# Four background conditionings moved from the grouped attention into the low-rank mixture, with their results kept in DRAM

## The reference, cut to what matters

```python
x = x + L1_ffn(cond2(x, side, side, w, u, t))    # low-rank mixture of experts, conditioning 3
x = x + L2_attn(cond(x, side, side, w, u, t))    # grouped attention, conditioning 4
x = x + L2_ffn(cond2(...))                       # quantised feed-forward, conditioning 5
x = x + L3_attn(cond(...))                       # selective scan, conditioning 6
x = x + L3_ffn(cond2(...))                       # mixture, four experts a token, conditioning 7

def cond(r, k, v, w, u, time_emb):
    decay = exp(-exp(w)) * (0.5 + 0.5 * tf)
    ek = exp(min(k, 30)); ekv = ek * v
    # a = a * decay + ekv_t, b = b * decay + ek_t: scans over the tokens, forward and backward
    num = nf + nb - ekv + exp(min(u + k, 30)) * v
    den = df + db - ek + exp(min(u + k, 30))
    return sigmoid(r) * (num / max(den, 1e-8)) * (0.8 + 0.2 * tf)
```

## Time and profile before

| | us |
|---|---|
| median of 3 runs (2028.22 to 2039.93) | 2029.68 |
| the profiled execution | 2035.18 |
| its span | 2033.9 |

### The profile page before, as it was taken

One profiled execution on the slowest core, in us unless ns is written; L12 is line 12 of the kernel. 1 busy time (PEld: TensorE's weight loads), 2 busy tenths in 40 slices (PEclk: granted clock), 3 DMA queues, 4 the chain that ended last, 5 costly groups with the idle time before them and its releaser, 6 DMA issues.

```text
span 2033.9 us, 16567 instructions
## 1 busy us (share of the span) xinstructions
PE 1648.3 (81%) x5375; PEld 885.9 (44%) x5386; DVE 1279.3 (63%) x2046; ACT 913.6 (45%) x1581; POOL 357.1 (18%) x233
## 2 busy tenths in 40 slices
PE   0599788878877999986798989876667777689998
PEld 0255354436753434433344444432312332247776
DVE  7476346634433653546778787748768799955665
ACT  4311525433332211225878787734555453324444
POOL 5000032223100010000000000000025665502332
PEclk9975789988676999998899999876778899989999
DMA  2000076426003000001101010100100000021110
GB/s 86 0 1 1 0 261 217 155 64 104 1 1 126 0 0 0 0 1 55 47 1 44 1 44 1 39 33 17 44 0 0 1 0 0 0 68 44 53 47 27
DMA packets 40043, 80.68 MB, mean 40 GB/s; under 512 B 8882, under 2 KB 26116, under 8 KB 37398
## 3 DMA queue, kind: packets, MB, share of 16 engines
q1 hardware_dynamic: 34870, 53.93, 8.7%
q0 software_dynamic: 5088, 25.69, 3.6%
HBM read 71.34 MB, written 7.22 MB: 39 GB/s over the span
## 4 chain that ended last, share of the span: by engine, by line
PE 29%; DVE 12%; ACT 7%; issue 4%; POOL 2%; DMA 0%; PEldq 0%; POOLq 0%; DVEq 0%; SPq 0%; ACTq 0%; PEld 0%
PE bank L157 21%; PE bank L2510 3%; PE bank L1895 2%; POOL s_bu L2426 2%; DVE s_bu L2322 1%; DVE s_bu L2314 1%; DVE g_q L1593 1%; DVE g_turn L1591 1%; DVE g_turn L1592 1%; PE bank L2446 1%; PE bank L1885 1%; PE bank L1876 1%; DVE g_q L1597 1%; DVE g_rs L1584 1%; DVE q_g L2070 1%
## 5 line engine op out<-in xcount | busy, mean ns | idle before, releaser
L2426 POOL TENSOR_TENSOR s_bu<-s_rep,s_du 128x1024 f32<-128x1024 f32 x64 | 151.5, 2371 | 718.0 <-DVE s_du L2306 607.7
L2314 DVE TENSOR_TENSOR_SCAN s_bu<-bank,s_bu 128x1024 f32<-128x1024 f32 x64 | 146.0, 2282 | 21.1 <-ACT bank L2388 10.1
L2510 PE MATMUL bank<-s_bu,ident 128*128 128x512 f32 x256 | 132.8, 645 | 1.0 <-DVE s_dl L2263 0.3
L2388 ACT ACTIVATE bank<-s_dl,s_an 128x510 f32<-128x510 f32 x128 | 83.0, 682 | 106.3 <-DVE s_bu L2314 106.2
L157 PE MATMUL bank<-e_xs,e_wsp 128*128 128x512 f32 x528 | 127.8, 391 | 0.7 <-issue 0.7
L157 PEld LDWEIGHTS bank<-e_xs,e_wsp 128*128 128x128 f32 x528 | 99.0, 188 | 22.8 <-issue 1.9
L157 PE MATMUL bank<-r_am,r_b 128*128 128x512 f32 x240 | 108.8, 593 | 0.0
L157 PE MATMUL bank<-conditioned,g_wqk 128*128 128x512 f32 x160 | 88.2, 680 | 7.4 <-DVE g_wqk L1578 7.4
L2446 PE MATMUL bank<-s_bc,s_pick 96*128 96x512 bf16 x128 | 42.0, 412 | 56.9 <-DVE s_bu L2322 55.5
L1420 POOL TENSOR_TENSOR r_ys<-r_y,r_y 128x512 f32<-128x512 f32 x14 | 22.8, 1631 | 342.0 <-DVE r_y L1365 342.0
L2322 DVE TENSOR_TENSOR s_bu<-s_bu,bank 128x1024 f32<-128x1024 f32 x64 | 76.7, 1199 | 4.3 <-PE bank L2446 4.2
(11 more groups left out here) (452 smaller groups left out, 3783.6 us busy)
## 6 DMA issues: line engine op xcount, KB each, us to landing
e_wgu<-in_e_gu SPq DMA_DIRECT2D x22, 256.0 KB, 2.7
b_vw<-b_values SPq DMA_DIRECT2D x48, 64.0 KB, 3.4
e_wd<-in_e_down SPq DMA_DIRECT2D x22, 128.0 KB, 2.6
r_w<-in_r_w SPq DMA_DIRECT2D x3, 896.0 KB, 8.2
g_wqk<-in_g_qk SPq DMA_DIRECT2D x4, 640.0 KB, 4.1
g_wgv<-in_g_gv SPq DMA_DIRECT2D x4, 640.0 KB, 4.4
g_wo<-in_g_wo SPq DMA_DIRECT2D x4, 512.0 KB, 3.6
m_sorted<-m_zero SPq DMA_DIRECT2D x1, 1920.0 KB, 12.8
```

The costliest lines, as they stand in the source:

```text
L2314: e.tensor_tensor_scan(b, flat(k.pairs[n % 2][:, :, :]), b, 0.0, ALU.mult, ALU.add).then_inc(k["s_scanned"].up(), 1)
L2388: e.activation(banks[2 * (n % 2) + i][:, :].rearrange("p (b t) -> p b t", t=T)[:, :, 1:T], m.dl[:, et, half(h)].rearrange("p (b t) -> p b ...
L2426: e.tensor_tensor(m.bu[n % m.NBU][:, :, :], m.rep[:, 2 * np:2 * np + 2, :], m.du[:, et, half(h)].unsqueeze(1).to_broadcast([P, 2, HALF]), ...
L2510: summed = e.matmul(banks[6][:, :], k.ident[:, :], m.bu[(n - 1) % m.NBU][:, i, :], start=np == 0 and i == 0, stop=np == m.NP - 1 and i == ...
```

## The change

The last four jobs, (6,0), (6,1), (7,0) and (7,1), move from the grouped attention into the low-rank mixture, where each half now runs four jobs instead of two: (4,0), (4,1), (6,0), (6,1), then (7,0), (7,1), (5,0), (5,1). `WKV_ORDER` and `wkv_count` number the semaphores in that order. The generators advance by 7 steps a unit; on VectorE 3 of them stand between the product and the weighting. The factors of 6 and 7 pass through slot 1, are stored to a DRAM tensor (four transfers of 512 KB) and read back into slots 2 and 0 in the grouped attention. The finishing products of 7 and 5 wait until the slot's earlier content is stored. All background calls leave the grouped attention.

```diff
+WKV_ORDER = (0, 1, 2, 3, 4, 6, 7, 5)
+KEPT = ((6, 0), (6, 1), (7, 0), (7, 1))
...
+        self.kept_factors = nc.dram_tensor("kept_factors", [len(KEPT), P, TOK], F32).ap()
...
+def wkv_count(l, ct):
+    return 2 * WKV_ORDER.index(l) + ct
...
 def wkv_finish(k, e, job):
     l, ct = job
-    j = 2 * l + ct
+    j = wkv_count(l, ct)
+    if l in (5, 7):
+        e.wait_ge(*k[f"factor_kept{ct}"].at(16 if l == 7 else 32))
     e.wait_ge(*k["wkv_inverse"].at(j + 1))
     e.wait_ge(*k["wkv_num"].at(j + 1))
-    e.tensor_tensor(k.factors[SLOT[l]][:, ct, :], k.nb[j % 2][:, :], k.db[j % 2][:, :], ALU.mult).then_inc(k["factor_ready"].up(), 1)
+    e.tensor_tensor(k.factors[1 if l > 4 else SLOT[l]][:, ct, :], k.nb[j % 2][:, :], k.db[j % 2][:, :], ALU.mult).then_inc(k["factor_ready"].up(), 1)
...
 def condition_vector(k, e, l):
-    e.wait_ge(*k["factor_ready"].at(2 * l + 2))
+    if l > 5:
+        e.wait_ge(*k[f"factor_back{l}"].at(32))
+    else:
+        e.wait_ge(*k["factor_ready"].at(wkv_count(l, 1) + 1))
...
+LORA_JOBS = ([(4, 0), (4, 1), (6, 0), (6, 1)], [(7, 0), (7, 1), (5, 0), (5, 1)])
...
@@ lora_sync
+    for n, (l, ct) in enumerate(KEPT):
+        e.wait_ge(*k["factor_ready"].at(wkv_count(l, ct) + 1))
+        e.dma_start(k.kept_factors[n], k.factors[1][:, ct, :]).then_inc(k[f"factor_kept{ct}"].up(16), 16)
...
@@ lora_vector
-        background = wkv_vector(k, e, [(4 + h, 0), (4 + h, 1)])
+        background = wkv_vector(k, e, LORA_JOBS[h])
...
             e.tensor_tensor(m.sl[i][:, :], m.sl[i][:, :], banks[b + 1][:, :], ALU.mult).then_inc(k["r_product"].up(), 1)
+            step(background, 3)
...
@@ lora_scalar
-        background = wkv_scalar(k, e, [(4 + h, 0), (4 + h, 1)])
+        background = wkv_scalar(k, e, LORA_JOBS[h])
...
-            step(background, 4)
+            step(background, 7)
...
@@ grouped_sync
+    for ct in range(CT):
+        e.wait_ge(*k[f"factor_kept{ct}"].at(32))
...
     for g in range(m.KV):
+        if g == 1:
+            e.wait_ge(*k["conditioned"].at(10))
+            for n, (l, ct) in enumerate(KEPT):
+                e.dma_start(k.factors[SLOT[l]][:, ct, :], k.kept_factors[n]).then_inc(k[f"factor_back{l}"].up(16), 16)
...
@@ grouped_vector
-    background = wkv_vector(k, e, [(6, 0), (6, 1), (7, 0), (7, 1)])
-                    run_out(background)
-            if new is not None and s < 6:
-                step(background, 2)
@@ grouped_scalar
-    background = wkv_scalar(k, e, [(6, 0), (6, 1), (7, 0), (7, 1)])
-            if new is not None and s < 6:
-                step(background, 2)
-    run_out(background)
```

## The result

| | before | changed |
|---|---|---|
| median of 12 runs, us | 2032.22 | 2045.33 |
| lowest and highest, us | 2027.34, 2039.93 | 2036.28, 2055.32 |
| span of the profiled execution, us | 2033.9 | 2045.2 |

The changed kernel is slower by the ratio 1.0059 (95% interval 1.0036 to 1.0082), 12 us. The direction was right and the time lies in the range of 2031 to 2076, but the point of 2053 was 8 us high: the loss is within 1%, which had a chance of 0.34 against 0.57 for more. The miss in the net is larger: +24 us forecast, +12 measured.

The account below looks back on a forecast made before the run. The prediction took TensorE to bound both stages. Low-rank mixture +42.6 us, grouped attention -18.5 and DRAM moves 0 summed to +24, giving 2053 us from a median of 2029.7, range 2031 to 2076.

Parts of the forecast that it names:

- the walk: Low-rank mixture: stepping the queues through one half gave 24.2 us of TensorE idle against 7.9, +16.3 a half.
- the signs that I had named: Right if mixture halves take about 123 to 130 us, grouped passes all near 49 and pass 1 near 45.
- The clock term: Low-rank mixture: TensorE's granted clock falls to 0.93, adding 5 us a half, bounds 0 and +12.6.
- The lower bound of +30: Low-rank mixture: the least it was to cost, in us, with +42.6 forecast and +58 as upper bound.
- Step (1): Start of the grouped attention: an Exp with its load before the first square goes, -1.9 us.
- Step (2): Grouped attention, pass 1: Ln and Exp with two loads ahead of the projections' variance and root go, -6.3 us.
- Step (3): Grouped attention, passes 3 and 5: an odd pass becomes like an even one, 53.2 to 49.3 us, -3.9 each.
- Step (4): Grouped attention, pass 7: between 1.5 and 4.7 us gained, taken as -2.5.
- The moves through DRAM: Four 512 KB stores and their reads cost 0 us; a transfer lands in 3.6 us, uncovered reads would cost 14.
- VectorE's slack taking it all: Rival, chance 0.13: extra mixture steps run in VectorE's idle 43.7 us a half, costing about 0; 2011 us.
- Background steps pacing the grouped attention: Rival, chance 0.14: in-order VectorE steps delay TensorE's rows; without them -32 us, 2040 us, or -59, 2013 us.
- The clock: Rival, chance 0.20, slower: idle pieces in the mixture lower TensorE's clock; 2068 us at 0.88, 2090 at most.

Follow-up runs that it names:

- first experiment: Kernel before without any background work in the grouped attention and nothing extra in the mixture: 2014.59 us against 2034.71, ratio 0.9912.
- the second experiment: Kernel before with ScalarE's background steps left out of the grouped attention, VectorE's all kept without waits for ScalarE: 2015.2 us, ratio 0.9914.
- the third experiment: Kernel before with ScalarE's Ln and Exp moved from unit 5 of odd grouped passes to unit 0 of the next pass: 2020.28 us, ratio 0.9938.
- the last: Kernel before, all jobs in place, ScalarE's background steps moved to other units in both stages: 2009.28 us against 2034.77, ratio 0.9868.

## Why the prediction was right or wrong

**The bound and the walk.** TensorE bounds both stages and loses time where its queue meets a late product: shown. All six waits of a half stand where the walk put them. Their sizes were 1.7, 2.7, 5.7, 2.2, 4.7 and 7.2 us, measured 1.5, 2.2, 5.3, 2.2, 4.7 and 5.35. The extra idle is 13.4 us a half where 16.3 stood. Of the signs that I had named, the halves (122.5 and 122.6 us) lie just under 123 to 130, the later passes near 49 as said (48.6 to 49.4), and pass 1 at 47.2 where I had 45.

**The clock term** was mis-sized, and with it the sum. I added 5 us a half to 16.3, 21.3 in all; the halves grew by 15.7 and 16.1 us (122.45 and 122.61 against 106.77 and 106.52 from first unit to last matmuls). The granted clock fell to 0.95, where I took 0.93, and the growth beyond the idle is 2.3 and 2.7 us where 5 stood. Part of the loss lay in the shadow of a wait: the last second product ran 3.78 us instead of 1.98 and ended at 759.56, while VectorE was held by the finishing product of a job, which waited for ScalarE's Exp:

```profile
759.82 1.23 DVE L234 TENSOR_TENSOR factor<-wkv_nb,wkv_db 128x1024 f32<-128x1024 f32 x1 [1.28 <-ACT wkv_db L248]
760.96 0.68 DVE L1389 TENSOR_TENSOR r_am<-r_maskx,bank 128x512 f32<-128x512 f32 x1
```

The low-rank sums (L1389 on) could start no sooner with a faster product. So the last wait came out 1.85 us shorter (5.35 against 7.2), and the two together were 9.13 us where the walk had 1.98 + 7.2. I had counted those microseconds twice, once as idle and once as clock. Low-rank mixture: +42.6 forecast; measured +31.8 in the two halves, and +29.8 to +33.9 in the whole stretch (the changed kernel and the one without DRAM), which differ ahead of the first unit. The lower bound of +30 was a slip: with no loss of clock at all my sum gives +32.6, and the halves came in below even that.

**The grouped attention.** -18.5 forecast, -16.5 measured, -16.9 for the background alone. Step (1), the first Exp, is right: from conditioning 4 to the first value copy it took 24.7 us before and 22.7 after. Step (2), pass 1, gave 3.8 instead of 6.3 us in the changed kernel (51.0 to 47.2) and 5.8 without the DRAM transfers (45.3 us):

```profile
1009.93:1055.21 45.28, 37.92 (x131) 20.20 (x130) 31.16 (x83) 37.17 (x84) 0.00 (x0) 0.96 0.10 34
```

The same instructions ran at 0.89 and 0.96 of the clock in the two, and the timelines part at one place: from 1028.8 on three groups of matmuls took 2.85, 2.08 and 1.92 us, and 1.96, 1.12 and 1.02 in the other, with 0.9 us of it covered by a shorter wait. So some 2 us of the step hang on the clock. It isn't the transfers: without any background and without them (first experiment) pass 1 took 47.2 us as well. Step (3), passes 3 and 5: -4.6 and -3.8 us, forecast -3.9 each. Step (4), pass 7 and behind it, is wrong in size: 2.5 forecast, 0.3 measured (88.7 to 88.4 us from the last value copy to conditioning 5). Without the extra work in the mixture the same stretch took 85.9 us, so what pass 7 is worth stays open within some 3 us. Passes 0, 2, 4 and 6, priced at nothing, gave 2.0 us together (41.7, 49.3, 49.3 and 49.2 us to 41.2, 49.2, 48.6 and 48.6), which nearly makes up for step (4). VectorE's steps at nothing: shown by the second experiment.

**The moves through DRAM** cost nothing, as forecast, though the four reads landed after 9.5 us in the median, not 3.6. They were issued within 2.2 us (from 943.50), right behind seven other loads, and the DMA engines were 0.90 to 1.02 busy until 950; which of these made them long was not tried. The factors were due 400 us later.

**The rivals.** VectorE's slack taking it all: refuted by the halves, 122.5 us with VectorE idle for 24. Background steps pacing the grouped attention: refuted, 443.7 us with all of them in place. The clock: it fell, but less than even the forecast had it, to 0.95 and not to 0.88. The point of the Trainium skill (ScalarE: Activation LUTs, What ACT_TABLE_LOAD costs) about a drain of over 1 us at each switch isn't borne out here: ScalarE's lines behind job 2 and in the third experiment show loads of 1.28 us, the activation 0.01 to 0.02 us behind them and the load as close behind what ran before. The measurement decides.

**Where the net went.** The change bought 17 us in the grouped attention with 30 to 34 us in the mixture. What was paid for in the grouped attention was mostly the place of four pairs of Ln and Exp, and moving the jobs away also moved the 68 us of VectorE work that had cost nothing there into a stage where it does cost.

## What to carry to other kernels

Before moving hidden work out of a stage, find which of its instructions is actually on the path: here 23 us of ScalarE work cost 17, and 68 us of VectorE work cost nothing, and one step moved past two units gave most of the gain without any price. Whether a queue has room is not told by its busy sum (99 of 122 us still stalled TensorE by 21) but by what stands in it, and where, between two results that the bound engine waits for: the same seven steps a unit cost 5 us a half more with three of them moved behind the weighting. And here a table-switching chain did least harm behind the unit whose successor was longest in coming.

## What the runs showed of the hardware

Lost clock and idle time did not add: TensorE's second product ran at the lower level (granted clock 0.50, 3.78 us against 1.98) where the wait behind it would have been as much longer otherwise. The same grouped stretch, with the same instruction counts, took 443.9 and 440.5 us at granted clocks of 0.90 and 0.92, and one pass of it 47.2 and 45.3 at 0.89 and 0.96. The first of each pair is the changed kernel, the second the one without the DRAM transfers; why their clocks differ was not tried. Nor does the mean clock of a pass tell its time: pass 1 took 46.3 us at 0.96 in the third experiment and 46.3 at 0.89 in the last. Stages ahead of the first edit, identical in both kernels, ended at 609.4 us in one profile and 605.8 in the other. GpSimd's add in the mixture took 1.9 us in the mean instead of 1.6 with VectorE fuller (1.6 in the median of both, at most 3.25 instead of 2.18), and 1.29 in the median with VectorE's steps cut to a few columns. So the two lengthen each other: an add of VectorE beside it took 2.11 us against 1.21. By what means was not tried.
